# A conv, attention and FFN block on one core: the second FFN bias into the fourth row tile, shifts turned in one product, v and projection by the whole array

## The reference

```
x = x + leaky_relu(sum over the 2 best of 5 experts of gate * (gn(x) @ We[e] + be[e]))
t = t + attn(ln(t)):  6 heads of 16, causal, 256 tokens per image
        wei = softmax(k q^T / sqrt(96)),  out = (wei v) @ wproj + bproj
t = t + ffn(ln(t)):   4 experts, 96 -> 384 -> 96, weights of the best 2 by softmax
        h = gelu(ln(t) @ w1[e] + b1[e]),  y[e] = h @ w2[e] + b2[e]
        out = sum over e of masked[e] * y[e]
```

## Time and profile before

| | us |
|---|---|
| median of three runs | 316.29 |
| profiled execution | 316.23 |
| its span | 314.5 |
| PE busy | 297.0 |
| DVE busy | 238.7 |
| ACT busy | 221.1 |
| POOL busy | 106.3 |

### The profile page before, as it was taken

One profiled execution on the slowest core, in us unless ns is written; L12 is line 12 of the kernel. 1 busy time (PEld: TensorE's weight loads), 2 busy tenths in 40 slices (PEclk: granted clock), 3 DMA queues, 4 the chain that ended last, 5 costly groups with the idle time before them and its releaser, 6 DMA issues.

```text
span 314.5 us, 9387 instructions
## 1 busy us (share of the span) xinstructions
PE 297.0 (94%) x3459; PEld 214.7 (68%) x3459; DVE 238.7 (76%) x1050; ACT 221.1 (70%) x441; POOL 106.3 (34%) x176
## 2 busy tenths in 40 slices
...
GB/s 178 185 41 0 1 120 72 113 83 125 101 82 115 4 45 0 4 96 113 36 81 95 4 3 77 128 31 14 87 112 3 29 27 44 0 10 62 2 27 25
DMA packets 28436, 18.70 MB, mean 59 GB/s; under 512 B 16820, under 2 KB 26952, under 8 KB 28392
## 3 DMA queue, kind: packets, MB, share of 16 engines
...
...
## 4 chain that ended last, share of the span: by engine, by line
PE 65%; SPq 2%; DMA 1%; ACT 1%; DVE 1%; issue 1%; POOL 1%; DVEq 0%; POOLq 0%; ACTq 0%
PE PS L1010 21%; PE PS L988 8%; PE PS L989 7%; PE PS L994 4%; PE PS L946 4%; PE PS L961 3%; PE PS L862 3%; PE PS L904 2%; PE PS L928 2%; PE PS L1003 2%; PE PS L854 2%; SPq L509 2%; PE PS L893 1%; DMA k_stack<-qk_parts 1%; PE PS L932 1%; PE PS L975 1%
## 5 line engine op out<-in xcount | busy, mean ns | idle before, releaser
L793 ACT ACTIVATE hidden<-PS,b_t 128x512 f32<-128x512 f32 x96 | 59.5, 683 | 33.1 <-PE PS L994 32.9
L1010 PE MATMUL PS<-w_f,hidden 128*64 128x96 f32 x1536 | 70.4, 248 | 0.0
L1010 PEld LDWEIGHTS PS<-w_f,hidden 128*64 128x64 f32 x1536 | 64.4, 137 | 7.0 <-issue 7.0
L1266 DVE SCALAR_TENSOR_TENSOR res<-PS,weight,res 128x96 f32<-128x96 f32 x128 | 31.4, 309 | 35.5 <-PE PS L1010 35.2
L988 PE MATMUL PS<-t_a,w_a 128*128 128x512 f32 x96 | 42.0, 437 | 0.0
L989 PE MATMUL PS<-t_b,w_b 128*128 128x512 f32 x96 | 37.9, 395 | 0.0
L1170 DVE CUSTOM_DVE_ANT_0 masked<-PS,causal 128x128 bf16<-128x128 f32 (+1 forms) x120 | 34.9, 352 | 3.6 <-PE PS L893 2.1
L769 ACT ACTIVATE prob_a<-PS 128x512 f32<-128x512 f32 x48 | 25.9, 601 | 10.8 <-PE PS L928 10.7
L654 POOL TENSOR_SCALAR_AFFINE_SELECT prob_a<-prob_a 128x768 f32<-128x768 f32 x16 | 13.8, 865 | 57.0 <-ACT prob_a L769 57.0
L1131 DVE SCALAR_TENSOR_TENSOR PS<-conv_y,weight,PS 128x96 f32<-128x96 f32 x128 | 30.2, 316 | 2.5 <-ACT PS L721 2.4
L575 POOL TENSOR_TENSOR ln_var<-ln_mv,eps_t 128x4 f32<-128x4 f32 x16 | 3.2, 198 | 74.6 <-DVE ln_mv L1063 74.6
...
## 6 DMA issues: line engine op xcount, KB each, us to landing
...
```

The lines of the kernel that those rows point to most:

```text
L793: act.activation(hidden[:, m, 0:T * P], PS[:, bank("ffn1", n, index), 0:T * P], ACT.Gelu, bias=b1_t[:, m:m + 1]).then_inc(act_emptied["ffn ...
L1010: mm = pe.matmul(PS[strip:strip + STRIP, y, t * C:(t + 1) * C], hidden[:, m, t * P + strip:t * P + strip + STRIP], w2_f[:, m, :], start=Fa ...
L1266: ins = dve.scalar_tensor_tensor(res2[:, t, :], PS[:, y, t * C:(t + 1) * C], weight1[:, t, e:e + 1], res2[:, t, :], ALU.mult, ALU.add).the ...
```

## The change

- b2's three parts lie in rows 96 to 98 of b2_parts, and the bias is a product of three input rows, in the fourth row tile. One load, one GpSimd row, and three SyncE transfers (a new step w_b2 at the head of SyncE's list) make them; the memsets go.
- rest1 stays a step of its own for expert 0. For experts 1 to 3 the rest products of expert e + 1 are sent at the start of ffn2.e, ahead of its bias. ffn2.e waits for its gelus only behind its bias.
- shift_parts is laid out part, head, tile; one product turns all 72 columns, ScalarE copies 72 rows of 128, and SyncE places 72 pieces.
- v and proj take WHOLE = 128 tokens for each product.
- All five lists are made anew. TensorE's has 82 filler products for 89. SyncE's has w_w1.0 and w_w1.1 both behind the stack copies of unit 2, ScalarE's has w_w1 earlier, GpSimd's has w_b2.2 ahead of xn@2.

The rest of the diff, without the lists, cut:

```diff
+WHOLE = P
...
-        shift_parts = sb("shift_parts", [P, TILES, SHIFT, HEADS], BF16)
-        shift_rest = sb("shift_rest", [P, TILES, HEADS])
-        shift_t = sb("shift_t", [SHIFT * HEADS, PT], BF16)
+        shift_parts = sb("shift_parts", [P, SHIFT, HEADS, TILES], BF16)
+        shift_rest = sb("shift_rest", [P, HEADS, TILES])
+        shift_t = sb("shift_t", [SHIFT * HEADS * TILES, P], BF16)
...
-        b2_f = hidden[0:65, 5, 0:E1 * C]
-        b2_rest = hidden[0:65, 6:8, 0:E1 * C]
-        b2_lead = hidden[0:65, 8, 0:E1 * C].bitcast(BF16).rearrange("p (a n) -> p a n", a=2)
+        b2_f = hidden[0:1, 5, 0:E1 * C]
+        b2_rest = hidden[0:1, 6:8, 0:E1 * C]
+        b2_lead = hidden[0:1, 8, 0:E1 * C].bitcast(BF16).rearrange("p (a n) -> p a n", a=2)
+        b2_last = hidden[0:1, 6, 0:E1 * C // 2].bitcast(BF16)
...
-            ffn_loads += [(b2_f[r:r + 1, :], b2.rearrange("(a e) c -> a (e c)", a=1)) for r in (0, 32, 64)]
+            ffn_loads.append((b2_f[:, :], b2.rearrange("(a e) c -> a (e c)", a=1)))
...
-                    sp.dma_start(k_stacks[n % 2][STACK:STACK + SHIFT, :, 0:T * P], shift_t[:, 0:T * P]).then_inc(shift_placed, 16)
+                    sp.dma_start(k_stacks[n % 2][STACK:STACK + SHIFT, :, :].rearrange("p h (a t) -> p (h a) t", t=P),
+                                 shift_t[:, :]).then_inc(shift_placed, 16)
...
+                elif kind == "w_b2":
+                    sp.wait_ge(b2_step, 4)
+                    sp.wait_ge(b2_split, 1)
+                    for i, part in enumerate((b2_lead[:, 0, :], b2_lead[:, 1, :], b2_last[:, :])):
+                        sp.dma_start(b2_parts[C + i:C + i + 1, :], part).then_inc(b2_placed, 16)
...
-                        pool.tensor_copy(b2_parts[0:1, :], b2_lead[0:1, 0, :]).then_inc(b2_split, 1)
-                        pool.wait_ge(b2_split, 1)
-                        pool.tensor_copy(b2_parts[32:33, :], b2_lead[32:33, 1, :]).then_inc(b2_split, 1)
-                        pool.wait_ge(b2_split, 2)
-                        pool.tensor_copy(b2_parts[64:65, :], b2_rest[64:65, 1, :]).then_inc(b2_split, 1)
-                        pool.wait_ge(b2_split, 3)
+                        pool.tensor_copy(b2_last[:, :], b2_rest[:, 1, :]).then_inc(b2_split, 1)
...
-                    act.activation(shift_t[:, 0:T * P], PS[0:SHIFT * HEADS, bank("shift", n), 0:T * P // 2].bitcast(BF16), ACT.Copy
+                    act.activation(shift_t[:, :], PS[0:SHIFT * HEADS * TILES, bank("shift", n), 0:P // 2].bitcast(BF16), ACT.Copy
...
+            def rest_rows(n, e):
+                T = size_of(n)[1]
+                for j in range(CHUNKS):
+                    rows = slice(j * REST, (j + 1) * REST)
+                    pe.matmul(PS[:, bank("ffn1", n, (e * CHUNKS + j,)), 0:T * P], w1_c[rows, e, :],
+                              t2_cs[n % T2][rows, 0:T * P], start=False, stop=True).then_inc(filled["ffn1"], 1)
...
                     for t in range(T):
-                        for strip in range(0, P, STRIP):
-                            rows = slice(t * P + strip, t * P + strip + STRIP)
-                            mm = pe.matmul(PS[strip:strip + STRIP, bank("v", n), t * C:(t + 1) * C], t1s[n % 2][:, rows],
+                        for strip in range(0, P, WHOLE):
+                            rows = slice(t * P + strip, t * P + strip + WHOLE)
+                            mm = pe.matmul(PS[strip:strip + WHOLE, bank("v", n), t * C:(t + 1) * C], t1s[n % 2][:, rows],
                                            wv_w[:, :], start=True, stop=True, skip_group_check=True)
...
                     wait_bank_free(pe, "shift", n)
                     pe.wait_ge(shift_ready, n + 1)
-                    for t in range(T):
-                        mm = pe.transpose(PS[0:SHIFT * HEADS, bank("shift", n), t * P // 2:(t + 1) * P // 2].bitcast(BF16),
-                                          shift_parts[:, t, :, :].rearrange("p a h -> p (a h)"), ident_b[:, :])
-                    mm.then_inc(filled["shift"], 1)
+                    pe.transpose(PS[0:SHIFT * HEADS * TILES, bank("shift", n), 0:P // 2].bitcast(BF16),
+                                 shift_parts[:, :, :, :].rearrange("p a h t -> p (a h t)"), ident_b[:, :]).then_inc(filled["shift"], 1)
...
-                                for strip in range(0, P, STRIP):
-                                    rows = slice(half * P + strip, half * P + strip + STRIP)
-                                    mm = pe.matmul(PS[strip:strip + STRIP, bank("proj", n), t * C:(t + 1) * C],
+                                for strip in range(0, P, WHOLE):
+                                    rows = slice(half * P + strip, half * P + strip + WHOLE)
+                                    mm = pe.matmul(PS[strip:strip + WHOLE, bank("proj", n), t * C:(t + 1) * C],
...
                 elif kind == "rest1":
-                    e = index[0]
-                    for j in range(CHUNKS):
-                        rows = slice(j * REST, (j + 1) * REST)
-                        pe.matmul(PS[:, bank("ffn1", n, (e * CHUNKS + j,)), 0:T * P], w1_c[rows, e, :],
-                                  t2_cs[n % T2][rows, 0:T * P], start=False, stop=True).then_inc(filled["ffn1"], 1)
+                    rest_rows(n, 0)
                 elif kind == "ffn2":
                     e = index[0]
                     if n == 0 and e == 0:
-                        pe.wait_ge(b2_split, 3)
-                    wait_act(pe, "ffn1", n, (CHUNKS * (e + 1) - 1,))
+                        pe.wait_ge(b2_placed, 16 * 3)
                     wait_bank_free(pe, "ffn2", n, index)
                     y = bank("ffn2", n, index)
-                    pe.matmul(PS[:, y, 0:T * C], ones_b[:, :],
-                              b2_parts[:, e * C:(e + 1) * C].unsqueeze(1).to_broadcast([P, T, C]),
+                    if e + 1 < E1:
+                        rest_rows(n, e + 1)
+                    pe.matmul(PS[:, y, 0:T * C], ones_b[C:C + 3, :],
+                              b2_parts[C:C + 3, e * C:(e + 1) * C].unsqueeze(1).to_broadcast([3, T, C]),
                               start=True, stop=False, skip_group_check=True)
+                    wait_act(pe, "ffn1", n, (CHUNKS * (e + 1) - 1,))
                     for t in range(T):
...
-            dve.memset(b2_f[:, :], 0.0).then_inc(conv_pads, 1)
-            dve.memset(b2_parts[:, :], 0.0).then_inc(pad_ready, 1)
...
-                    lead = shift_parts[:, 0:T, 0, :]
-                    step_done(dve.tensor_scalar(lead, row_max[:, 0:T, :], -1.0, None, ALU.mult))
+                    maxima = row_max[:, :, :].rearrange("p t h -> p h t")
+                    lead = shift_parts[:, 0, :, :]
...
```

More of the change, by code:

```diff
@@ L56 @@
     PE: """
[L57 to L86, removed]
@@ new lines @@
+        prob.1.4@0:5 shift@1:0 qk.1@2:4 pv.0@0:3 pv.1@0:5 warm.3@9:0 prob.0.0@1:0 prob.0.1@1:2 prob.0.2@1:1
+        prob.0.3@1:6 conv.2@5:4 conv.3@5:0 prob.0.4@1:3 prob.1.0@1:2 proj@0:1 prob.1.1@1:4 prob.1.2@1:5 prob.1.3@1:6
+        v@2:3 warm.5@10:2 score.0.0@2:2 score.0.1@2:1 score.0.2@2:4 score.0.3@2:5 prob.1.4@1:6 score.0.4@2:2
+        norm2_t@0:1 score.1.0@2:6 score.1.1@2:4 score.1.2@2:5 pv.0@1:2 pv.1@1:6 gate2@0:4 score.1.3@2:5 score.1.4@2:1
+        conv.0@6:0 norm1_t@3:2 ffn1.0@0:5 ffn1.1@0:3 ffn1.2@0:1 rest1.0@0:-1 proj@1:2 qk.0@3:6 shift@2:5 qk.1@3:3
@@ new lines @@
+        rest1.0@1:-1 qk.0@4:2 qk.1@4:6 ffn1.3@1:4 shift@3:0 proj@2:3 ffn1.4@1:5 ffn1.5@1:0 ffn2.0@1:1 ffn1.6@1:2
+        ffn1.7@1:4 ffn1.8@1:5 ffn1.9@1:0 ffn2.1@1:3 ffn1.10@1:1 ffn1.11@1:6 norm2_t@2:2 ffn2.2@1:4 prob.0.0@3:5
+        prob.0.1@3:0 prob.0.2@3:2 prob.0.3@3:1 gate2@2:3 conv.0@7:6 conv.1@7:4 conv.2@7:5 conv.3@7:0 prob.0.4@3:2
+        score.0.0@4:6 score.0.1@4:4 prob.1.0@3:3 prob.1.1@3:5 v@3:0 score.0.2@4:1 score.0.3@4:2 prob.1.2@3:6
+        score.0.4@4:3 score.1.0@4:4 prob.1.3@3:0 prob.1.4@3:1 v@4:5 ffn1.0@2:6 ffn1.1@2:2 ffn1.2@2:0 score.1.1@4:1
@@ L160 @@
-        weights@5 shift@7 att.0@6 ffn2.2@4 att.1@6 ffn2.3@4 proj@6 ffn2.0@5 norm2_t@6 att.0@7 gate2@6 att.1@7 ffn2.1@5
-        proj@7 weights@6 ffn2.2@5 ffn2.3@5 ffn2.0@6 norm2_t@7 ffn2.1@6 ffn2.2@6 gate2@7 weights@7 ffn2.3@6 ffn2.0@7
-        ffn2.1@7 ffn2.2@7 ffn2.3@7
+        gmean@2 gates.0@2 mix.4@1 qk.0@0 qk.1@0 xadd@1 stats1@1 gates.1@2 mix.1@2 gvar@2 mix.2@2 mix.3@2 mix.4@2 xadd@2
+        gates.0@3 score.0.0@0 score.0.1@0 gates.1@3 qk.0@1 qk.1@1 score.0.2@0 score.0.3@0 stats1@2 score.0.4@0 mix.1@3
@@ new lines @@
+        gates.1@5 xadd@4 ffn2.0@0 ffn2.1@0 stats1@4 mix.1@5 mix.2@5 ffn2.2@0 mix.3@5 mix.4@5 norm2_t@1 score.0.0@3
+        score.0.1@3 ffn2.3@0 score.0.2@3 score.0.3@3 score.0.4@3 score.1.0@3 gate2@1 score.1.1@3 score.1.2@3
+        score.1.3@3 score.1.4@3 shift@3 att.0@2 att.1@2 gates.0@6 qk.0@4 weights@1 gates.1@6 proj@2 ffn2.0@1 xadd@5
+        qk.1@4 mix.1@6 stats1@5 mix.2@6 mix.3@6 mix.4@6 norm2_t@2 ffn2.1@1 ffn2.2@1 gate2@2 weights@2 score.0.0@4
```

(1 more changed line is left out.)

182 lines of the change are left out of this document (97 added, 85 removed).

## The result

| | before | after |
|---|---|---|
| median, us (executions) | 316.20 (20) | 322.01 (20) |
| lowest to highest, us | 314.67 to 318.94 | 317.59 to 323.10 |
| ratio after / before, 95% interval | | 1.0103 [1.0065, 1.0140] |
| profiled execution: time, span, us | 316.23, 314.5 | 317.59, 315.8 |
| granted clock, mean over the span | 0.998 | 1.0 (0.979 to 1.0 over the 20) |

The forecast was 311.1, with a range up to 316.0; the time lies above it. The ratio leaves out disturbed executions (over 1.5% above the fastest), here the seven longest, and so is less than the quotient of the medians, 1.018; a second series of the same kernel, beside 24 new executions of before, gave 1.0175 [1.0141, 1.0208].

The account below looks back on a forecast made before the run. TensorE was taken to bound the kernel from norm2_t@0 on. Terms -4.1 - 1.0 - 4.4 + 4.0 - 0.5 + 0.6 (two more score steps) + 0.3 = -5.1 took 316.2 to 311.1 us; range 306.5 to 316.

Parts of the forecast that it names:

- What bounds the kernel: From norm2_t@0 (84.7 us) on, TensorE is busy 224.16 of 226.20 us; what it saves there is saved.
- Bias in the fourth row tile, -4.1: Second FFN's b2 products: 24 of 32 hide beside the rest products in row tiles, 0.17 us each, -4.1 us.
- Rival 2: b2 runs after the rest products, not beside them; the 4.1 us isn't saved, 315.2 us; chance 0.13.
- Turned shift, -1.0: Shift on TensorE: four bf16 products become one, 0.056 us each, six units in the stretch, -1.0 us.
- Arrangement and whole-array passes, -4.4 and +4.0: TensorE: 57 fewer arrangement changes, five more leaving row tiles, -4.4 us; v and proj passes paced by 0.11 us loads, +4.0.
- Rivals 1 and 4: v and proj whole-array weight loads: hidden, 307.1 us, chance 0.15 (1); load and streaming in sequence, 323.3 us, chance 0.08 (4).
- Start-up, -0.5: Ahead of norm2_t@0: 82 fillers for 89 and an earlier qk@0, -0.5 us (-2 to +1).
- The lists, "+0.3 in all": Rest of block e+1 goes out inside ffn2.e, so its three gelus start later, costing +0.3 us in all.
- Rival 3: The remade lists wait: one gelu late at eight of 24 blocks, 4.6 us, 315.7 us; chance 0.16.
- The change leaves no long pause, so I give the clock no part: Granted clock, 1.00 throughout before, is taken to stay so; no time is allotted to it.

Follow-up runs that it names:

- the fastest kernel: Kernel before, its old lists, with bias in fourth row tile, one-product shift, strips kept, row-tile products of eight blocks moved directly ahead of ffn2 steps: 313.19 us, ratio 0.9874.

## Why the prediction was wrong, step by step

- *What bounds the kernel*: right for before. That what TensorE saves is then saved was right for the old lists (-3.2 us, the fastest kernel) and wrong for the new ones, where VectorE has 27% of the chain.
- *Bias in the fourth row tile, -4.1*: right, and for 28 biases, not 24. It starts 0.01 us behind the row tiles and adds nothing; taken out of them it costs 5.3 in one execution at the full clock, with the changes of arrangement. Rival 2 is out, as the fourth tile adds nothing to three (0.42 us and 0.43). The Trainium skill (TensorE: Matmul & The Clock Gate, Measured speedup vs the span model) has 3.07 times the speed for four row tiles of 512 columns; the loss of 1.7 us that the prediction estimated from it did not come, but no run here sets four such tiles against one, as the fourth has three rows and 384 columns.
- *Turned shift, -1.0*: right in TensorE's list (0.06 for 0.32, a change of arrangement included); alone -0.65 in the medians, interval up to 0, and -2.2 at the full clock, so if anything too small.
- *Arrangement and whole-array passes, -4.4 and +4.0*: the prices hold. The whole array alone gave +2.1 where the terms give +2.0; passes stand 0.109 to 0.116 apart. Rivals 1 and 4 are out. TensorE's busy time in the stretch fell by 3.1; the sum has 4.9 less. The missing 1.8 need not be work that did not come: the estimate of 1.5 to 1.9 us of pause that counts as busy in 11 more waits is as large. The runs don't split it further. By its own prices of 0.09 and 0.11 the range of the arrangement term is -4.1 to -5.3, not -4.0 to -5.0.
- *Start-up, -0.5*: right, norm2_t@0 at 84.3 instead of 84.7.
- *The lists, "+0.3 in all"*: **this step failed.** It stands at +4.8: idle 6.83 for 2.04 us, and nearer to +6.5 with the estimate of pauses that count as busy. Rival 3 named the place but the wrong mechanism: not gelu's late rows but VectorE's results (XT, res, shift_parts, t_b) and a normed row. The argument against it, that ScalarE has 69 us free in the stretch, was one on averages, and of VectorE's order nothing was asked. The counts of steps per list were compared, not what stands ahead of the step that each TensorE step waits for.
- *"The change leaves no long pause, so I give the clock no part"*: **this step failed too.** No long pause came; three waits of 0.4 to 0.8 us near 174, 183 and 194 us were enough in most executions, and the stretch at 0.50 behind it costs about 4.5 us (322.06 against 317.59). The Trainium skill (TensorE: Matmul & The Clock Gate, A second HAM failure mode: psum-queue depth-cycling) tells of a kernel whose frequent short idle gaps between groups of products made the clock go back and forth, at a loss of throughput. The runs agree in that short waits are enough: with four fillers (1.0 us) in one of these waits the clock kept 0.989 or more in 12 of 12 executions.

The account, in executions at the full clock: forecast 311.1, idle time +4.5 more than the 0.3, busy time +1.8 more (by the estimate above pauses too), the rest 0.2, makes 317.6. To 322.0, the median, it is the clock.

What stays open: which of the reorderings makes the waits (the lists of TensorE, VectorE and ScalarE were all remade, and they were exchanged only together), and what decides, from equal waits (2.95 and 2.96 us busy between 192 and 196), whether the clock falls.
